# A convolution-attention block and a group-normed attention on one core: rows for the second attention's residual taken by transposing x1, GpSimd's sums dropped, and the third image's z_hat placed earlier

## The chip, the cores and the metric

One NeuronCore of a Trainium2 chip runs the whole kernel in one launch. The metric is the device time in microseconds (us), the median over the runs shown. The engines are named as in the profile: PE (TensorE, matrix products and transposes), PEld (its weight loads), DVE (VectorE), ACT (ScalarE), POOL (GpSimd), SP (SyncE, which issues the DMA transfers). Each engine works through its own list of instructions in order; semaphores make one engine wait for another.

## What is computed

The input x has 4 images of 16 x 16 pixels with 128 channels, all in float32. Two layers follow each other. The second half of the first layer and the second layer are what matters here:

```
# layer 0, after its deformable attention has given att
z    = att @ mo_w + mo_b + x
z_ln = layernorm(z, ln_g, ln_b)                    # per pixel, over 128 channels
x1   = gelu(z_ln @ mlp_w + mlp_b) + z
# layer 1
xg   = groupnorm(x1, 32 groups of 4 channels, per image) * gn_gamma + gn_beta
q, k, v = xg @ wq + bq, xg @ wk + bk, xg @ wv + bv
attn = softmax(q @ k.T / sqrt(128))                # 256 x 256 per image
out  = (attn @ v) @ wo + bo + x1
```

## The kernel before

All is written by hand, engine by engine, so the order of the text is the order of execution on each engine, and semaphores tie the engines together. An image is 256 pixels, that is two tiles of 128 pixels (rows on the partitions); there are 8 such tiles. The first attention runs tile by tile in a pipeline that takes until about 50 us of the span. What follows goes image by image, b = 0 to 3.

For each image: `z_tile` (L631) adds the projected attention and the input on DVE, with pixels on the partitions. `z_stats`, `z_aggr` and `z_var` (L636 to L646) take mean and variance over the channels, `z_scale` (L314) raises the variance to the power -1/2 on POOL, and `zhat_image` (L648) normalises two tiles on DVE. `z_transpose` (L1002) on PE transposes both z (columns 256 to 511 of a PSUM bank) and z_hat (columns 0 to 255) so that channels lie on the partitions; `zt_image` (L440) copies z_hat's transpose to SBUF on ACT, `mlp_image` (L1020) multiplies it by the MLP's weights, `gelu_image` (L444) applies gelu on ACT and gives gel_t, and `x1_image` (L653) on DVE adds the transposed z to it: x1_t, channels on the partitions.

Two users take x1. The group norm needs x1_t: `gn_stats`, `gn_aggr` on DVE, then on PE `gn_mean` (L1071), on DVE `gn_square` (L700), on PE `gn_spread` (L1083), on DVE `gn_var` (L706), on POOL `gn_pow` (L326), and on DVE `norm_image` (L712), which writes x_gn. This chain runs twice, for images 0 and 1 together (n = 0) and for images 2 and 3 (n = 1). From x_gn, `project_qk` (L1092) on PE and `project_out` (L719) on DVE make q and k.

The residual of the last line needs x1 with pixels on the partitions. Before, `gelu_transpose` (L1065) transposes gel_t back on PE, `residual` (L319) adds z and the output bias on POOL (z_res), and `x1_residual` (L658) on DVE adds the two: x1_res. It also frees the PSUM bank for q and k, so `project_qk(0)` and `(1)` wait for it, and `score_image(0)` and `(1)` (L1115) wait for x1_residual(2) and (3).

`keep_warm(2, 6)` (L812) issues two matmuls on a constant tile whose result nobody reads. The lists of calls that set the order stand at the end of each engine's block: L746 to L805 for DVE, L1150 on for PE, L332 to L345 for POOL. The bias sits in out_bias, written by ACT at L461.

Of the kernel before, what the change touches and what calls it, by code (L numbers as in the profile page):

```python
# [11 lines left out]
P = 128  # L12
B, H, W, C = 4, 16, 16, 128
HW = H * W
S = HW // P
T = B * S
# [52 lines left out]
def build(nc, x, early, fold, mid, late, rows, ln_rows, out):  # L69
    ctx = ExitStack()  # L70
    with ctx:
        def sb(name, shape, dt=F32):
            return ctx.enter_context(nc.sbuf_tensor(name, shape, dt))
# [25 lines left out]
        def r(name):  # L99
# [23 lines left out]
        out_bias = sb("out_bias", [P, C])  # L123
# [24 lines left out]
        z = sb("z", [P, T, C])  # L148
# [5 lines left out]
        z_t = sb("z_t", [P, T, P])  # L154
        gel_t = sb("gel_t", [P, B, HW])
        x1_t = sb("x1_t", [P, B, HW])
        z_res = sb("z_res", [P, T, C])
        x1_res = sb("x1_res", [P, T, C])
        gst = sb("gst", [P, B, 6])
        gmv = sb("gmv", [P, B, 2])  # L160
# [23 lines left out]
            "sampling": "coord_mm tanh_ok dx_ok dy_ok fx_ok ay_ok hx_ok hy_ok bilin_ok interp_mm sampled_ok",  # L184
            "queries, keys, values": "qh_mm qh_ok k_mm k_ok kblk_ok kblk_p v_mm v_even v_odd",
            "attention": """s_mm smax_ok ssub_ok pt_mm exp_ok av_mm recip_ok att_ok attt_mm attt_ok msa_mm xres_ok z_ok""",
            "norm of z and MLP": "zst_ok zmv_ok zve_ok zrs_ok zhat_ok zt_mm zt_ok mlp_mm gel_ok zres_ok x1t_ok gelt_mm x1res_ok",
            "group norm": "gst_ok gmv_ok dev_mm dev2_ok gvar_mm gve_ok gmean_ok grs_ok xgn_ok",
            "second attention": """qk_mm q1_ok k1_ok v1_mm v1_ok s1_mm nmax1_ok p1_ok p1t0_mm p1t1_mm p1t0_ok p1t1_ok
                av1_mm rec1_ok y_ok y_out""",  # L190
# [76 lines left out]
        @block.gpsimd  # L267
        def _(pool):
            pool.memset(warm[:, :], 0.0).then_inc(s["warm_set"], 1)  # L269
            pool.memset(ones_row[:, :], 1.0)  # L270
            pool.memset(ones_col[:, :], 1.0).then_inc(s["ones_set"], 1)
            pool.memset(eps[:, :], LN_EPS)
            pool.memset(neg_half[:, :], -0.5).then_inc(s["consts"], 1)
            pool.memset(v1[:, :, :, C:C + 1], 1.0).then_inc(s["v1ones_set"], 1)
            pool.memset(v_blk[:, :, :, 0:2 * HD], 0.0)
            pool.wait_ge(s["early_in"], 16)
            pool.wait_ge(s["hat_ok"], 4)
            for n in range(0, len(SHIFTS), WD_CHUNK):
                taps = w("dw_q")[:, n * PHASES:(n + WD_CHUNK) * PHASES]
                pool.tensor_tensor(wd[:, n:n + WD_CHUNK].rearrange("p n k j -> p (n k) j"),  # L280
                                   w("ident32").unsqueeze(1).to_broadcast([P, WD_CHUNK * PHASES, BLK]),
                                   taps.unsqueeze(2).to_broadcast([P, WD_CHUNK * PHASES, BLK]), ALU.mult).then_inc(s["wd_ok"], 1)

            def norm_affine(h):

                t = halves(h)

                pool.wait_ge(s["hat_a" if h else "hat_ok"], 4)
                pool.wait_ge(s["lnrow_in"], 16)
                pool.tensor_tensor(x_g[:, t], x_hat[:, t], gb[:, 0:C].unsqueeze(1).to_broadcast([P, 4, C]), ALU.mult).then_inc(s["xg_ok"], 1)  # L290
                pool.wait_ge(s["xg_ok"], h + 1)
                pool.tensor_tensor(x_ln[:, t], x_g[:, t], gb[:, C:2 * C].unsqueeze(1).to_broadcast([P, 4, C]), ALU.add).then_inc(s["xln_ok"], 1)

            norm_affine(0)
            pool.wait_ge(s["mid_in"], 16)
            pool.tensor_copy(v_blk[:, :, :, 2 * HD:VW],
                             w("ones_mask").unsqueeze(1).unsqueeze(1).to_broadcast([P, B, PAIRS, 2])).then_inc(s["vones_set"], 1)
            norm_affine(1)

            pool.wait_ge(s["bilin_ok"], G)  # L300
            pool.wait_ge(s["msabias_ok"], 1)
            pool.wait_ge(s["xst_in"], 16)
            pool.tensor_tensor(x_res[:, :, :], x_st[:, :, :].rearrange("p b (s c) -> p (b s) c", s=S),  # L303
                               msa_bias[:, :].unsqueeze(1).to_broadcast([P, T, C]), ALU.add).then_inc(s["xres_ok"], 1)

            for b in range(G, B):
                pool.wait_ge(s["k_ok"], 1)
                pool.tensor_tensor(k_blk[:, b], k_t[:, b].unsqueeze(1).to_broadcast([P, NH, PIX]),
                                   w("head_of").unsqueeze(2).to_broadcast([P, NH, PIX]), ALU.mult).then_inc(s["kblk_p"], 1)

            pool.wait_ge(s["late_in"], 16)
            pool.tensor_scalar(mlp_wg[:, :], w("mlp_w"), w("ln_g"), None, ALU.mult).then_inc(s["mlpw_ok"], 1)

            def z_scale(b):  # L314

                pool.wait_ge(s["zve_ok"], b + 1)
                pool.tensor_tensor(zrs[:, 2 * b:2 * b + 2], zve[:, 2 * b:2 * b + 2], neg_half[:, 0:2], ALU.pow).then_inc(s["zrs_ok"], 1)  # L317

            def residual(b):  # L319

                pool.wait_ge(s["z_ok"], 2 * b + 2)
                pool.wait_ge(s["outbias_ok"], 1)
                pool.tensor_tensor(z_res[:, 2 * b:2 * b + 2, :], z[:, 2 * b:2 * b + 2, :],
                                   out_bias[:, :].unsqueeze(1).to_broadcast([P, S, C]), ALU.add).then_inc(s["zres_ok"], 1)

            def gn_pow(n):  # L326

                i = slice(GN_SETS[n].start, GN_SETS[n].stop)
                pool.wait_ge(s["gve_ok"], n + 1)
                pool.tensor_tensor(grs[:, i], gve[:, i], neg_half[:, i], ALU.pow).then_inc(s["grs_ok"], 1)  # L330

            z_scale(0)  # L332
            pool.tensor_scalar(wq1g[:, :], w("wq1"), w("gn_gamma"), None, ALU.mult)
            pool.tensor_scalar(wk1g[:, :], w("wk1"), w("gn_gamma"), None, ALU.mult)
            pool.wait_ge(s["w_vo_ok"], 1)
            pool.tensor_scalar(w_vog[:, :], w_vo[:, :], w("gn_gamma"), None, ALU.mult).then_inc(s["gamma_ok"], 1)
            z_scale(1)
            residual(0)
            residual(1)
            z_scale(2)  # L340
            z_scale(3)
            gn_pow(0)
            residual(2)
            residual(3)
            gn_pow(1)  # L345

        @block.scalar
# [162 lines left out]
        def _(dve):  # L510
# [137 lines left out]
            def zhat_image(b):  # L648
                dve.wait_ge(s["zrs_ok"], b + 1)
                for i in (2 * b, 2 * b + 1):  # L650
                    dve.tensor_scalar(z_hat[:, i], z[:, i], zmv[:, i, 0:1], zrs[:, i:i + 1], ALU.subtract, ALU.mult).then_inc(s["zhat_ok"], 1)

            def x1_image(b):  # L653

                dve.wait_ge(s["gel_ok"], b + 1)
                dve.tensor_tensor(x1_t[:, b], gel_t[:, b], zt_bank(b)[:, HW:2 * HW], ALU.add).then_inc(s["x1t_ok"], 1)  # L656

            def x1_residual(b):  # L658
                dve.wait_ge(s["gelt_mm"], b + 1)
                dve.wait_ge(s["zres_ok"], b + 1)  # L660
                dve.tensor_tensor(x1_res[:, 2 * b:2 * b + 2], bank[3 + b][:, HW:2 * HW].rearrange("p (s c) -> p s c", s=S),
                                  z_res[:, 2 * b:2 * b + 2], ALU.add).then_inc(s["x1res_ok"], 1)

            max_tile(0)
            shift_tile(0)
# [26 lines left out]
            def gn_stats(b):  # L692
                dve.wait_ge(s["x1t_ok"], b + 1)
                dve.bn_stats(gst[:, b], x1_t[:, b]).then_inc(s["gst_ok"], 1)  # L694
# [62 lines left out]
            x1_image(0)  # L757
            z_tile(T - 2)
            x1_image(1)
            gn_stats(0)  # L760
            gn_stats(1)
            z_tile(T - 1)
# [5 lines left out]
            z_aggr(T - 1)  # L768
            z_var(3)
            gn_square(0)  # L770
            zhat_image(2)
            x1_residual(0)
            gn_var(0)
            zhat_image(3)

            norm_image(0)
            norm_image(1)
            x1_residual(1)
            x1_image(2)
            gn_stats(2)  # L780
            project_out(0)
            x1_residual(2)
            x1_image(3)
            gn_stats(3)
            gn_aggr(2)
            gn_aggr(3)
            x1_residual(3)
            gn_square(1)
            project_out(1)
            gn_var(1)  # L790
            max_image(0)
            norm_image(2)
# [15 lines left out]
        def _(pe):  # L808
# [253 lines left out]
                if i == 2:  # L1062
                    fold_second()

            def gelu_transpose(b):  # L1065
                pe.wait_ge(s["gel_ok"], b + 1)
                for t in range(S):
                    m = pe.transpose(bank[3 + b][:, HW + t * P:HW + (t + 1) * P], gel_t[:, b, t * P:(t + 1) * P], w("ident"))
                m.then_inc(s["gelt_mm"], 1)

            def gn_mean(n):  # L1071

# [116 lines left out]
            att_transpose(T - 1)  # L1189
            keep_warm(2, 6)  # L1190
            out_project(T - 1)
            gelu_transpose(0)
            gelu_transpose(1)
            keep_warm(2, 6)
            gn_mean(0)
            keep_warm(2, 6)
            gn_spread(0)
            z_transpose(2)
            z_transpose(3)
            mlp_image(2)  # L1200

            project_qk(0)
            mlp_image(3)
            gelu_transpose(2)
            project_v(0)
            gelu_transpose(3)
            project_qk(1)
            gn_mean(1)
            score_image(0)
            gn_spread(1)  # L1210
            project_v(1)
# [81 lines left out]
```

## Time and profile before

| | before |
|---|---|
| median of 3 runs | 79.3 us (78.77, 79.3, 79.84) |
| the profiled execution, its own time | 79.27 us |
| its span, first to last instruction | 77.4 us |
| PE busy | 70.6 us (91%) |
| DVE busy | 51.7 us (67%) |
| ACT busy | 33.9 us (44%) |
| POOL busy | 24.3 us (31%) |
| granted PE clock | 1.000 over the span |

The span is the time from the first to the last instruction in the trace; the execution's own time is 1.87 us more than that. A busy PE is not a PE at its peak: its matmuls are pipelined and overlap, so successive ones of 128 columns in float32 start 0.11 us apart though each lasts 0.27 us. A DVE instruction likewise starts a little before the record of the one ahead ends. In rows of a timeline several like instructions are merged ("x2"), and the time is from the first's start to the last's end. The name x_t in the trace is the tile x1_t, x_res stands for x_res and x1_res, q and k for q1 and k1, dev for dev2, and so on, since numbers are left out.

### The profile page before, as it was taken

The numbers are of one execution on the slowest core, as the hardware profiler recorded it, in microseconds if no ns is written. First come the engines' busy times: TensorE is split into PE (matmuls) and PEld (weight loads), VectorE is DVE, ScalarE is ACT, GpSimd is POOL, SyncE is SP. The second block draws the span as 40 slices with busy tenths as digits, with TensorE's granted clock in tenths as the row PEclk, the third lists the DMA queues.
The fourth block names the chain that finished last, engine by engine and source line by source line (L and its number), as shares of the span: only waits on it lengthen the run. The fifth ranks groups of instructions, "written<-read, shape, count | busy, mean of one in ns | idle before, by whom it ended". The sixth has DMA issues, their size and how long they took to land.

```text
span 77.4 us, 1968 instructions
## 1 busy us (share of the span) xinstructions
PE 70.6 (91%) x732; PEld 53.6 (69%) x732; DVE 51.7 (67%) x172; ACT 33.9 (44%) x84; POOL 24.3 (31%) x37
## 2 busy tenths in 40 slices
PE   4999699998999999999999999998897999998950
PEld 2345599783786647879777989845485869996830
DVE  0478742116366959477789968599799786868480
ACT  6112397068139563524424419820248048263600
POOL 5008999900000038390019137123820030000000
PEclk9999999999999999999999999999999999999999
DMA  0789870000000000000000000000000000010112
GB/s 9 226 270 150 305 289 12 0 8 0 0 8 0 0 0 4 0 0 8 0 0 0 4 0 0 8 0 0 0 0 0 0 0 4 0 68 9 59 55 89
DMA packets 3051, 3.07 MB, mean 40 GB/s; under 512 B 225, under 2 KB 2657, under 8 KB 3042
## 3 DMA queue, kind: packets, MB, share of 16 engines
q1 hardware_dynamic: 3042, 2.95, 12.8%
q8 instruction: 6, 0.10, 0.5%
q14 instruction: 3, 0.02, 0.1%
HBM read 2.42 MB, written 0.52 MB: 38 GB/s over the span
## 4 chain that ended last, share of the span: by engine, by line
PE 63%; DVE 17%; issue 5%; DMA 5%; ACT 3%; SPq 2%; POOL 2%; DVEq 0%; POOLq 0%; ACTq 0%
PE bank L810 53%; DMA x_hw<-x 5%; PE bank L971 5%; PE bank L1140 2%; DVE smax L604 2%; DVE x_t L656 1%; DVE gst L694 1%; SPq L247 1%; DVE st L528 1%; DVE bilin L578 1%; DVE x_gn L716 1%; DVE dist_y L562 1%; PE bank L989 1%; DVE q_conv L517 1%; POOL grs L330 1%
## 5 line engine op out<-in xcount | busy, mean ns | idle before, releaser
L810 PE MATMUL bank<-k_blk,qh 128*128 128x512 f32 x16 | 8.4, 605 | 0.0
L810 PE MATMUL bank<-v_blk,p_t 128*128 128x34 f32 x64 | 7.8, 267 | 0.0
L810 PEld LDWEIGHTS bank<-v_blk,p_t 128*128 128x128 f32 x64 | 7.8, 192 | 0.0
L810 PE MATMUL bank<-warm 128*128 128x512 bf16 x18 | 6.3, 471 | 1.0 <-POOL warm L269 1.0
L604 DVE TENSOR_REDUCE smax<-bank 128x8 f32<-128x512 f32 x8 | 5.5, 685 | 2.4 <-PE bank L810 2.4
L317 POOL TENSOR_TENSOR zrs<-zve,neg_half 128x2 f32<-128x2 f32 x4 | 2.9, 714 | 12.7 <-DVE zve L646 12.7
L810 PE MATMUL bank<-q_ph,wd 128*32 128x112 f32 (+5 forms) x256 | 6.8, 249 | 0.0
L303 POOL TENSOR_TENSOR x_res<-x_st,msa_bias 128x1024 f32<-128x1024 f32 x1 | 2.4, 2358 | 12.8 <-DVE bilin L578 12.8
L431 ACT ACTIVATE p_t<-bank 128x512 f32<-128x512 f32 x8 | 4.8, 597 | 3.4 <-PE bank L971 3.4
L810 PEld LDWEIGHTS bank<-q_ph,wd 128*32 128x32 f32 x256 | 5.6, 109 | 0.7 <-issue 0.3
L611 DVE TENSOR_TENSOR s_sub<-bank,smax 128x512 f32<-128x512 f32 x8 | 5.5, 682 | 0.1
L280 POOL TENSOR_TENSOR wd<-pack_early 128x512 f32<-128x512 f32 x4 | 4.1, 1046 | 4.4 <-DVE x_hat L540 4.4
L810 PE MATMUL bank<-v,p_t 128*128 128x129 f32 x32 | 4.8, 284 | 0.6 <-ACT p_t L233 0.4
L810 PEld LDWEIGHTS bank<-v,p_t 128*128 128x128 f32 x32 | 4.2, 190 | 1.2 <-issue 1.0
L971 PE MATMUL bank<-pack_early,s_sub 128*128 128x128 f32 x32 | 5.0, 279 | 0.0
L488 ACT ACTIVATE p<-bank,nmax 128x256 f32<-128x256 f32 x8 | 3.4, 476 | 3.0 <-DVE nmax L728 2.8
L438 ACT COPY att_t<-bank 128x128 f32<-128x128 f32 x8 | 2.1, 263 | 5.4 <-PE bank L989 5.3
L971 PEld LDWEIGHTS bank<-pack_early,s_sub 128*128 128x128 f32 x32 | 3.7, 144 | 0.8 <-issue 0.5
L810 PE MATMUL bank<-k,q 128*128 128x256 f32 x16 | 4.2, 385 | 0.0
L528 DVE BATCH_NORM_STATS2 st<-x_hw 128x6 f32<-128x128 f32 x8 | 1.8, 283 | 3.2 <-DMA x_hw<-x 3.2
L810 PEld LDWEIGHTS bank<-warm 128*128 128x128 bf16 x18 | 2.0, 122 | 2.9 <-issue 1.9
L810 PE MATMUL bank<-pack_mid,att_t 128*128 128x128 f32 x16 | 3.7, 311 | 0.2 <-DVE z L634 0.2
(149 smaller groups left out, 161.2 us busy)
## 6 DMA issues: line engine op xcount, KB each, us to landing
x_st<-x SPq DMA_DIRECT2D x1, 512.0 KB, 6.7
pack_late<-late SPq DMA_DIRECT2D x1, 448.0 KB, 7.3
out<-y SPq DMA_DIRECT2D x3, 128.0 KB, 1.7
pack_fold<-fold SPq DMA_DIRECT2D x1, 320.0 KB, 4.1
pack_mid<-mid SPq DMA_DIRECT2D x1, 261.0 KB, 5.8
x_hw<-x SPq DMA_DIRECT2D x2, 128.0 KB, 2.2
x_hw<-x SPq DMA_DIRECT2D x1, 256.0 KB, 3.8
pack_early<-early SPq DMA_DIRECT2D x1, 184.0 KB, 2.5
```

Of the source, the lines that this page charges most:

```text
L280: pool.tensor_tensor(wd[:, n:n + WD_CHUNK].rearrange("p n k j -> p (n k) j"), w("ident32").unsqueeze(1).to_broadcast([P, WD_CHUNK * PHASES ...
L303: pool.tensor_tensor(x_res[:, :, :], x_st[:, :, :].rearrange("p b (s c) -> p (b s) c", s=S), msa_bias[:, :].unsqueeze(1).to_broadcast([P, ...
L317: pool.tensor_tensor(zrs[:, 2 * b:2 * b + 2], zve[:, 2 * b:2 * b + 2], neg_half[:, 0:2], ALU.pow).then_inc(s["zrs_ok"], 1)
L431: act.activation(p_t[:, i % 2].rearrange("p j q -> p (j q)"), bank[5 + i % 2][:, :], ACT.Exp).then_inc(s["exp_ok"], 1)
L438: act.copy(att_t[:, i % 2], bank[0][:, 0:P]).then_inc(s["attt_ok"], 1)
L488: act.activation(p1[:, b % 2, t], bank[5 + b % 2][:, t * HW:(t + 1) * HW], ACT.Exp, bias=nmax1[:, 2 * b + t:2 * b + t + 1]).then_inc(s["p1 ...
L528: dve.bn_stats(st[:, i], x_hw[:, i]).then_inc(s["stats"], 1)
L604: dve.tensor_reduce(smax[:, i % 2], scores(i), AX.X, ALU.max).then_inc(s["smax_ok"], 1)
L611: dve.tensor_tensor(s_sub[:, i % 2], scores(i), smax[:, i % 2].unsqueeze(2).to_broadcast([P, NH, PIX]), ALU.subtract).then_inc(s["ssub_ok" ...
L810: return pe.matmul(o, l, r_, start=start, stop=stop, **k)
L971: m = pe.transpose(bank[5 + i % 2][:, j * P:(j + 1) * P], s_sub[:, i % 2, 2 * j:2 * j + 2].rearrange("p h q -> p (h q)"), w("ident"))
L1140: m = pe.transpose(bank[(2, 0)[t]][:, j * P:(j + 1) * P], p1[:, b % 2, t, j * P:(j + 1) * P], w("ident"))
```

## The change

Three things are changed; no other line moves.

- `residual` is gone from POOL, and z_res with it. `gelu_transpose` becomes `x1_transpose`: PE transposes x1_t, not gel_t, and so has to wait for x1_image on DVE, not for gelu on ACT. `x1_residual` adds out_bias, broadcast over the two tiles.
- On DVE `zhat_image(2)` moves from behind `gn_square(0)` to ahead of `gn_stats(0)`; `x1_image(2)` moves from behind `x1_residual(1)` to ahead of `norm_image(0)`; `x1_residual(2)` and `x1_residual(3)` move behind `gn_aggr(3)` and `project_out(1)`.
- On PE `z_transpose(2)` goes ahead of `gn_mean(0)`, `mlp_image(2)` ahead of `gn_spread(0)`, in the place of one `keep_warm(2, 6)`; `mlp_image(3)` goes ahead of `project_qk(0)`; the transposes of images 2 and 3 for the residual go behind `project_v(0)` and `gn_mean(1)`.

```
-            def residual(b):
-                pool.wait_ge(s["z_ok"], 2 * b + 2)
-                pool.wait_ge(s["outbias_ok"], 1)
-                pool.tensor_tensor(z_res[:, 2 * b:2 * b + 2, :], z[:, 2 * b:2 * b + 2, :],
-                                   out_bias[:, :].unsqueeze(1).to_broadcast([P, S, C]), ALU.add).then_inc(s["zres_ok"], 1)
             z_scale(1)
-            residual(0)
-            residual(1)
             z_scale(2)
             z_scale(3)
             gn_pow(0)
-            residual(2)
-            residual(3)
             gn_pow(1)
...
             def x1_residual(b):
-                dve.wait_ge(s["gelt_mm"], b + 1)
-                dve.wait_ge(s["zres_ok"], b + 1)
+                dve.wait_ge(s["x1rows_mm"], b + 1)
+                dve.wait_ge(s["outbias_ok"], 1)
                 dve.tensor_tensor(x1_res[:, 2 * b:2 * b + 2], bank[3 + b][:, HW:2 * HW].rearrange("p (s c) -> p s c", s=S),
-                                  z_res[:, 2 * b:2 * b + 2], ALU.add).then_inc(s["x1res_ok"], 1)
+                                  out_bias[:, :].unsqueeze(1).to_broadcast([P, S, C]), ALU.add).then_inc(s["x1res_ok"], 1)
...
-            def gelu_transpose(b):
-                pe.wait_ge(s["gel_ok"], b + 1)
+            def x1_transpose(b):
+                pe.wait_ge(s["x1t_ok"], b + 1)
                 for t in range(S):
-                    m = pe.transpose(bank[3 + b][:, HW + t * P:HW + (t + 1) * P], gel_t[:, b, t * P:(t + 1) * P], w("ident"))
-                m.then_inc(s["gelt_mm"], 1)
+                    m = pe.transpose(bank[3 + b][:, HW + t * P:HW + (t + 1) * P], x1_t[:, b, t * P:(t + 1) * P], w("ident"))
+                m.then_inc(s["x1rows_mm"], 1)
...
             x1_image(1)
+            zhat_image(2)
             gn_stats(0)
```

Three places in the order of instructions. First PE between the transposes for the residual of images 0 and 1 and the fourth image's z_hat. Before:

```order
L1068 MATMUL bank<-pack_early,gel_t 128x128 x4
L810 MATMUL bank<-warm 128x512 x2
L810 MATMUL bank<-gmv,pack_late 128x2
L810 MATMUL bank<-warm 128x512 x2
L810 MATMUL bank<-gmv,pack_late 128x2
L810 MATMUL bank<-dev,pack_late 128x2
L810 MATMUL bank<-gmv,pack_late 128x2
L1014 MATMUL bank<-pack_early,z 128x128 x2
L1017 MATMUL bank<-pack_early,z_hat 128x128 x2
```

The same place of the change:

```order
L1055 MATMUL bank<-pack_early,x_t 128x128 x4
L797 MATMUL bank<-warm 128x512 x2
L1001 MATMUL bank<-pack_early,z 128x128 x2
L1004 MATMUL bank<-pack_early,z_hat 128x128 x2
L797 MATMUL bank<-gmv,pack_late 128x2
L797 MATMUL bank<-z_t,mlp_wg 128x256
L797 MATMUL bank<-gmv,pack_late 128x2
L797 MATMUL bank<-dev,pack_late 128x2
L797 MATMUL bank<-gmv,pack_late 128x2
L1001 MATMUL bank<-pack_early,z 128x128 x2
L1004 MATMUL bank<-pack_early,z_hat 128x128 x2
L797 MATMUL bank<-z_t,mlp_wg 128x256
```

The third image's transposes and MLP now stand on both sides of the first group norm matmul (gmv), and the second pair of warm matmuls is gone.

Second, PE around the first projection to q and k (x_gn with wq1g and wk1g) up to the first scores (k,q). Before:

```order
L810 MATMUL bank<-x_gn,wq1g 128x256
L810 MATMUL bank<-x_gn,wk1g 128x256
L810 MATMUL bank<-z_t,mlp_wg 128x256
L1068 MATMUL bank<-pack_early,gel_t 128x128 x2
L810 MATMUL bank<-w_vog,x_gn 128x128 x2
L1068 MATMUL bank<-pack_early,gel_t 128x128 x2
L810 MATMUL bank<-x_gn,wq1g 128x256
L810 MATMUL bank<-x_gn,wk1g 128x256
L810 MATMUL bank<-gmv,pack_late 128x2
L810 MATMUL bank<-k,q 128x256 x2
```

The same place of the change, from the fourth image's MLP on:

```order
L797 MATMUL bank<-z_t,mlp_wg 128x256
L797 MATMUL bank<-x_gn,wq1g 128x256
L797 MATMUL bank<-x_gn,wk1g 128x256
L797 MATMUL bank<-w_vog,x_gn 128x128 x2
L1055 MATMUL bank<-pack_early,x_t 128x128 x2
L797 MATMUL bank<-x_gn,wq1g 128x256
L797 MATMUL bank<-x_gn,wk1g 128x256
L797 MATMUL bank<-gmv,pack_late 128x2
L1055 MATMUL bank<-pack_early,x_t 128x128 x2
L797 MATMUL bank<-k,q 128x256 x2
```

The fourth image's MLP moved ahead of x_gn's first product, and the last transpose moved behind the second group norm matmul, directly ahead of the scores.

Third, DVE from the variance of the last two z tiles (zve) to the first q. Before:

```order
L646 TENSOR_SCALAR zve<-zmv 128x2
L704 TENSOR_SCALAR dev<-bank 128x1 x2
L651 TENSOR_SCALAR z_hat<-z,zmv,zrs 128x128 x2
L661 TENSOR_TENSOR x_res<-bank,z_res 128x256
L709 TENSOR_SCALAR gve<-bank 128x2
L710 COPY gmean<-bank 128x2
L651 TENSOR_SCALAR z_hat<-z,zmv,zrs 128x128 x2
L716 TENSOR_SCALAR x_gn<-x_t,gmean,grs 128x256 x2
L661 TENSOR_TENSOR x_res<-bank,z_res 128x256
L656 TENSOR_TENSOR x_t<-gel_t,bank 128x256
L694 BN_STATS gst<-x_t 128x6
L722 TENSOR_SCALAR q<-bank,cols 128x256
```

The same place of the change:

```order
L634 TENSOR_SCALAR zve<-zmv 128x2
L692 TENSOR_SCALAR dev<-bank 128x1 x2
L649 TENSOR_TENSOR x_res<-bank,out_bias 128x256
L697 TENSOR_SCALAR gve<-bank 128x2
L698 COPY gmean<-bank 128x2
L639 TENSOR_SCALAR z_hat<-z,zmv,zrs 128x128 x2
L644 TENSOR_TENSOR x_t<-gel_t,bank 128x256
L704 TENSOR_SCALAR x_gn<-x_t,gmean,grs 128x256 x2
L649 TENSOR_TENSOR x_res<-bank,out_bias 128x256
L682 BN_STATS gst<-x_t 128x6
L710 TENSOR_SCALAR q<-bank,cols 128x256
```

The first z_hat pair of this list left for a place seven rows further up, and the third image's x_t came ahead of x_gn.

## Rows read from the trace of the kernel before

**Rows 1.** The page: PE's busy time, and its granted clock in 40 slices.
```profile
PE 70.6 (91%) x732; PEld 53.6 (69%) x732; DVE 51.7 (67%) x172; ACT 33.9 (44%) x84; POOL 24.3 (31%) x37
PEclk9999999999999999999999999999999999999999
```

**Rows 2.** The chain that ended last, in order: start us, us, what.
```profile
54.47 0.80 POOL grs L330
...
56.02 0.81 DVE x_gn L716
...
57.87 0.47 DVE q L722
...
60.12 3.33 PE bank L810 x20
...
63.46 0.80 PE bank L1140 x4
...
72.39 0.22 PE bank L1140 x2
```

**Rows 3.** Timeline, z_hat, z_res and x_gn: start us, us, engine, line, op [idle before].
```profile
46.09 1.12 DVE L651 TENSOR_SCALAR z_hat<-z,zmv,zrs 128x128 f32<-128x128 f32 x2 [0.64 <-POOL zrs L317]
...
46.40 1.41 POOL L323 TENSOR_TENSOR z_res<-z,out_bias 128x256 f32<-128x256 f32 x2 [0.34 <-ACT out_bias L461]
...
47.93 0.38 PE L1017 MATMUL bank<-pack_early,z_hat 128*128 128x128 f32 x2
...
55.22 1.45 POOL L323 TENSOR_TENSOR z_res<-z,out_bias 128x256 f32<-128x256 f32 x2
...
55.36 1.46 DVE L716 TENSOR_SCALAR x_gn<-x_t,gmean,grs 128x256 f32<-128x256 f32 x2 [0.40 <-POOL grs L330]
...
63.12 0.73 DVE L716 TENSOR_SCALAR x_gn<-x_t,gmean,grs 128x256 f32<-128x256 f32 x2 [0.22 <-POOL grs L330]
```

**Rows 4.** DVE's groups, first x_gn of each pair: xcount | busy us, mean ns | idle.
```profile
L716 DVE TENSOR_SCALAR x_gn<-x_t,gmean,grs 128x256 f32<-128x256 f32 x1 | 0.7, 731 | 0.4 <-POOL grs L330 0.4
...
L716 DVE TENSOR_SCALAR x_gn<-x_t,gmean,grs 128x256 f32<-128x256 f32 x1 | 0.4, 412 | 0.2 <-POOL grs L330 0.2
```

**Rows 5.** Timeline of the first group norm, 50 to 54.4 us.
```profile
50.06 0.70 POOL L317 TENSOR_TENSOR zrs<-zve,neg_half 128x2 f32<-128x2 f32 x1 [2.26 <-DVE zve L646]
...
50.84 0.41 DVE L656 TENSOR_TENSOR x_t<-gel_t,bank 128x256 f32<-128x256 f32 x1
...
52.02 0.24 DVE L698 BATCH_NORM_AGGREGATE gmv<-gst 128x2 f32<-128x6 f32 x2
...
52.96 0.34 DVE L704 TENSOR_SCALAR dev<-bank 128x1 f32<-128x1 f32 x2
...
53.23 0.59 DVE L651 TENSOR_SCALAR z_hat<-z,zmv,zrs 128x128 f32<-128x128 f32 x2
...
54.23 0.16 DVE L709 TENSOR_SCALAR gve<-bank 128x2 f32<-128x2 f32 x1
```

**Rows 6.** Timeline from the fourth image's z_hat to the first scores.
```profile
54.37 0.59 DVE L651 TENSOR_SCALAR z_hat<-z,zmv,zrs 128x128 f32<-128x128 f32 x2
...
55.02 0.44 PE L1017 MATMUL bank<-pack_early,z_hat 128*128 128x128 f32 x2
...
56.15 0.70 PE L810 MATMUL bank<-x_gn,wq1g 128*128 128x256 f32 x2 [0.26 <-DVE x_gn L716]
...
56.30 0.36 ACT L442 COPY z_t<-bank 128x256 f32<-128x256 f32 x1
...
56.68 0.59 PE L810 MATMUL bank<-x_gn,wk1g 128*128 128x256 f32 x2
...
57.08 0.40 DVE L656 TENSOR_TENSOR x_t<-gel_t,bank 128x256 f32<-128x256 f32 x1
57.12 0.59 PE L810 MATMUL bank<-z_t,mlp_wg 128*128 128x256 f32 x2
...
58.64 0.41 DVE L661 TENSOR_TENSOR x_res<-bank,z_res 128x256 f32<-128x256 f32 x1
```

More of the change, by code:

```diff
@@ L156, in build @@
         x1_t = sb("x1_t", [P, B, HW])
-        z_res = sb("z_res", [P, T, C])
         x1_res = sb("x1_res", [P, T, C])
@@ L186, in build @@
             "attention": """s_mm smax_ok ssub_ok pt_mm exp_ok av_mm recip_ok att_ok attt_mm attt_ok msa_mm xres_ok z_ok""",
-            "norm of z and MLP": "zst_ok zmv_ok zve_ok zrs_ok zhat_ok zt_mm zt_ok mlp_mm gel_ok zres_ok x1t_ok gelt_mm x1res_ok",
+            "norm of z and MLP": "zst_ok zmv_ok zve_ok zrs_ok zhat_ok zt_mm zt_ok mlp_mm gel_ok x1t_ok x1rows_mm x1res_ok",
             "group norm": "gst_ok gmv_ok dev_mm dev2_ok gvar_mm gve_ok gmean_ok grs_ok xgn_ok",
@@ L770, in _ @@
             gn_square(0)
-            zhat_image(2)
             x1_residual(0)
@@ L774, in _ @@
             zhat_image(3)
+            x1_image(2)
             norm_image(0)
@@ L778, in _ @@
             x1_residual(1)
-            x1_image(2)
             gn_stats(2)
             project_out(0)
-            x1_residual(2)
             x1_image(3)
@@ L786, in _ @@
             gn_aggr(3)
-            x1_residual(3)
+            x1_residual(2)
             gn_square(1)
             project_out(1)
+            x1_residual(3)
             gn_var(1)
@@ L1191, in _ @@
             out_project(T - 1)
-            gelu_transpose(0)
-            gelu_transpose(1)
+            x1_transpose(0)
+            x1_transpose(1)
             keep_warm(2, 6)
+            z_transpose(2)
             gn_mean(0)
-            keep_warm(2, 6)
+            mlp_image(2)
             gn_spread(0)
-            z_transpose(2)
             z_transpose(3)
-            mlp_image(2)
+            mlp_image(3)
             project_qk(0)
-            mlp_image(3)
-            gelu_transpose(2)
             project_v(0)
-            gelu_transpose(3)
+            x1_transpose(2)
             project_qk(1)
             gn_mean(1)
+            x1_transpose(3)
             score_image(0)
```

## The prediction

> **What bounds the kernel now.** I read the page's parts first: PE is busy for 91% of the span at full granted clock [rows 1]. A busy PE says little here, so the chain that ended last comes next. The reader is to see where it changes engine. Up to about 50 us it is PE, from 60.12 us on PE again, in pieces of 3.33 and 0.80 us with nothing between them [rows 2]. Between the two it runs over DVE and POOL: grs, x_gn, q, then PE's 60.12. The change works in these ten microseconds, and behind 60.12 us it alters nothing but one transpose pair. So I ask when the matmul that starts at 60.12 us (gn_mean(1), the first of the 20) starts after the change, and what stands between it and the first scores. The timeline gives the times.
>
> **POOL's sums.** The four z_res of `residual` go. POOL itself waits most of the time, so their time on POOL is worth nothing. What they do to DVE is: the z_hat pair that runs beside z_res takes 1.12 us, a pair without it 0.59 [rows 3, 5]; the x_gn pair beside z_res takes 1.46 us, the later pair 0.73 [rows 3], the first of each pair 731 and 412 ns [rows 4]. The Trainium skill, page "SBUF — State Buffer", tells that VectorE and GpSimd share one pair of ports, which an instruction of the tensor_scalar kind in its two-port form takes for its whole length, so that the other blocks; by that rule the slowing ends with the sums, and the trace agrees (1.46 against 0.73 us).
>
> Where is it on the path? The z_hat pair at 46.09 us ends at 47.21, and PE takes it only at 47.93 [rows 3]: 0.72 us of slack, worth nothing. The x_gn pair lies on the chain: 0.73 us less for the pair, 0.32 for its first (0.731 − 0.412).
>
> **z_hat(2) moves ahead of the group norm.** It needs zrs, ready at 50.76 (50.06 + 0.70), and it stands behind x1_image(1), which ends at 51.25 [rows 5]: no new wait. Two z_hat take 0.59 us less an overlap of 0.09, so 0.50 us. Behind it are queued gn_stats, gn_aggr (gmv), z_stats, z_var and gn_square (dev), with PE waiting for gmv and dev. DVE has no gap there, so all of it comes 0.50 us later: gmv at 52.76, dev over at 53.80 instead of 53.30. On PE, z_transpose(2) (four products 0.11 apart, 0.44 us) starts behind the warm matmuls at about 52.1 and is over by 52.8, when gmv arrives: free. mlp_image(2) needs two products of 0.22 us and an ACT copy (0.36) between 52.8 and 53.8: it fits ahead of gn_spread(0), which waits for dev. So gve starts at 54.73 instead of 54.23, and grs (0.80 us long) is ready at 55.76 instead of 55.26 [rows 2, 5].
>
> **What DVE does beside grs.** DVE was idle for 0.40 us ahead of x_gn [rows 3]. Now z_hat(3) (54.87 to 55.46) and x1_image(2) (0.33 of its own, to 55.79) fill the wait for grs. x_gn(0) runs from 55.86, with 0.10 for the semaphore as now, to 56.27, x_gn(1) to 56.60. Before, the two ended at 56.09 (55.36 + 0.731) and 56.83 (56.02 + 0.81) [rows 2 to 4]. The first is 0.18 later, the second 0.23 earlier.
>
> **The fourth image on PE.** mlp_image(3) now stands ahead of project_qk(0) in PE's queue. Its inputs: z_hat(3) is over at 55.46 instead of 54.96; PE's transposes run from 55.52 to 55.96 (before 55.02, 0.44 long); the ACT copy takes 0.36 behind that, to 56.37; mlp starts at 56.43 and takes 0.44 of PE, the distance from 56.68 to 57.12 [rows 6]. So project_qk(0) does not start at 56.32, when x_gn(0) would let it, but at 56.87, against 56.15 now. Its two products took from 56.15 to 57.27 (56.68 + 0.59); packed, 0.44 + 0.59, they end at 57.90 [rows 6]. Behind this wait stand project_v(0), the transposes for image 2, project_qk(1) and gn_mean(1) on PE, and project_out(0) on DVE.
>
> **DVE up to the second group norm.** x1_residual(1) and gn_stats(2) are over by 57.25, since x1_image(2) is already done. project_out(0) then waits for PE and starts at about 57.95 instead of 57.87: DVE, which was the bound, now idles 0.7 us, and here most of what x_gn gave back is lost. From there to gmv nothing differs but x1_residual(2), moved behind gn_aggr(3): 0.33 us less (58.64 to 58.97, where x1_image(3) began) [rows 6]. gn_mean(1) comes at 60.12 + 0.08 − 0.33 = 59.87.
>
> **Behind gn_mean(1).** The transpose pair of x1_t for image 3 now lies directly ahead of score_image(0). It costs 0.22 us, like any pair of transposes [rows 2]. Before, the pair stood where PE waited for DVE anyway, so nothing is given back for it. score_image(0) also waits for x1_residual(2), over at 60.14, which this covers. Net: −0.25 + 0.22 = −0.03 us. x1_residual(3), moved behind project_out(1), is over at about 61.8, and score_image(1), which waits for it, starts after 62.3. The rest repeats what it was.
>
> **Edits at nothing.** x1_residual adds out_bias instead of z_res: again one PSUM and one SBUF operand of the same size, 0.41 us [rows 6]. Bounds: 0 and, if the broadcast cost as much as the 0.32 us that the sharing cost, +0.3 for each of two that PE waits for. I take 0, by the nearest row. x1_transpose(0) and (1) wait for x1_image, over at 50.72 and 51.25; PE reaches them at 51.3 and 51.5 behind out_project(7): covered by 0.2 us. The two warm matmuls that go filled a wait: worth nothing while the clock stays.
>
> **Sum.** −0.03 us; against the profiled execution's own 79.27 us that is 79.24, 0.06 below the median of the runs shown (79.3). I say 79.2.
>
> **Rivals.**
>
> *More is kept (faster).* If z_hat(3), its copy and mlp_image(3) ran 0.4 us earlier, project_qk(0) would start at 56.32 and project_out(0) at 57.49 (56.32 + 0.53 + 0.59 + 0.05), 0.46 us sooner, and all behind it follows: 79.24 − 0.46 = 78.8. For it: ACT is idle there and copies take 0.36 at once. Against: z_hat(3) stands behind gn_var(0), which is 0.50 late. The ceiling, if all slowing of DVE by POOL lay on the path, is 0.53 + 0.73 = 1.26 us, so 78.0; that is still less than 2%.
>
> *The queues lose more (slower).* z_hat(2)'s 0.50 us runs through to gn_mean(1), and the transpose pair's 0.22 comes on top. The place is project_qk(0) behind mlp_image(3): beyond 56.87 us each later start reaches project_out(0) one for one, since DVE is then idle. It decides from 0.03 us of further delay on. An ACT copy or PE's transposes late by 0.3 to 0.5 us give 79.5 to 79.8. For it: three hand-overs (DVE to PE, PE to ACT, ACT to PE) now lie in a row ahead of project_qk(0), where none did. Against: each has its price in the rows, and I counted them.
>
> *The clock falls (slower).* Two of the warm matmuls go, and PE now waits at 55.0 to 55.5, 55.96 to 56.43 and about 59.1 to 59.8. The granted clock is full in all slices [rows 1], also through the waits from 53.2 to 56.2 and at 59.6 to 60.1. If it fell to the lower level through one stretch such as the 3.33 us piece [rows 2], this piece would take twice as long: 79.24 + 3.3 = 82.5. The Trainium skill, page "TensorE: Matmul & The Clock Gate", Part 4, states that transposes do not keep the clock up as matmuls do, which speaks against putting transposes where warm matmuls were. By that rule this rival would come true; the trace does not test it, since no stretch at the low level is in it.
>
> **Numbers.** Forecast (79.0 to 79.5) 0.55; more is kept (78.4 to 79.0) 0.20; the queues lose more (79.5 to 80.1) 0.20; the clock 0.04; an unnamed gain beyond 78 0.01. The range leaves out the ends: 78.5 to 80.0; the likeliest case's own is 79.0 to 79.5. It takes in the bound of x1_residual (+0.6 at most, 79.8). Two per cent, about what a measurement of this kernel tells from no change, is 1.6 us, that is 77.7 and 80.9. Only the unnamed gain passes the one, only the clock and a rest of the queues the other: faster 0.02, same 0.93, slower 0.05.
>
> **What the profile of the change would show.** x_gn's pair about 0.73 us long both times; z_hat(2) right behind x1_image(1), and gmv near 52.8; grs ending near 55.8 without an idle DVE ahead of x_gn; PE's mlp(3) directly ahead of wq1g at 56.4 and 56.9; DVE idle for about 0.7 us ahead of the first q; gn_mean(1) near 59.9, and the scores near 60.3. Wrong would be: x_gn still at 0.7 or 0.8 us each (the sharing was not the cause), a clock below 1.000, or the first q before 57.6 or after 58.2.

## The result and the profile after the change

| | before | after |
|---|---|---|
| median | 79.34 us (4 runs, 78.77 to 79.84) | 80.62 us (4 runs, 80.14 to 81.83) |
| ratio after / before | | 1.014, 95% interval 1.009 to 1.019 |
| profiled execution: span, granted PE clock | 77.4 us, 1.000 | 80.0 us, 0.956 |

The change made the kernel 1.4% slower. The forecast was 79.2 us with a range of 78.5 to 80.0, so the time lies outside. Ratios here and below leave out executions more than 1.5% above the fastest of their kernel, here the one of 81.83 us. The profiled execution of the change is the slowest of its four (81.83 us), so a second trace, of an execution of 80.7 us, is read beside it (e9_change_again, below). The other three of the four had a granted clock of 0.974, 0.974 and 0.978 over their spans.

The page of the changed kernel, busy time and granted clock in 40 slices of 2 us:

```profile
PE 73.0 (91%) x730; PEld 55.7 (70%) x730; DVE 50.5 (63%) x172; ACT 33.9 (42%) x84; POOL 21.4 (27%) x33
...
PEclk9999999999999999999999999999555899999999
```

The row of fives is what the kernel before does not have [rows 1]: from 55.9 to 62.7 us (read in stretches of 0.2 us) TensorE ran at the lower of its two levels, 1.2 GHz instead of 2.4. The chain that ended last (start us, us, what) shows what this did:

```profile
55.06 0.16 DVE gve L697
...
55.28 0.52 DVE z_hat L639 x2
...
55.85 0.70 PE bank L1004 x2
...
56.58 0.38 ACT z_t L430
...
57.00 3.78 PE bank L797 x10
60.78 0.43 PE bank L1055 x2
61.21 1.78 PE bank L797 x6
62.99 0.27 PE bank L1055 x2
63.27 2.85 PE bank L797 x18
66.11 0.01 issue
66.12 0.80 PE bank L1127 x4
```

Before, the ten microseconds up to 60.12 lay on DVE and POOL [rows 2]. Now ten matmul instructions from 57.00 on (five float32 products, each recorded as two) take 3.78 us and stand on the chain themselves. The timeline of the same kernel gives single instructions (start us, us, engine, line, op, shapes, idle before):

```profile
56.19 0.73 DVE L704 TENSOR_SCALAR x_gn<-x_t,gmean,grs 128x256 f32<-128x256 f32 x2
...
57.00 1.22 PE L797 MATMUL bank<-z_t,mlp_wg 128*128 128x256 f32 x2 [0.46 <-ACT z_t L430]
...
58.02 1.06 PE L797 MATMUL bank<-x_gn,wq1g 128*128 128x256 f32 x2
...
58.87 1.06 PE L797 MATMUL bank<-x_gn,wk1g 128*128 128x256 f32 x2
...
59.97 0.48 DVE L710 TENSOR_SCALAR q<-bank,cols 128x256 f32<-128x256 f32 x1 [2.37 <-PE bank L797]
...
62.71 0.28 PE L797 MATMUL bank<-gmv,pack_late 128*128 128x2 f32 x2
```

The x_gn pair takes 0.73 us, as forecast, where it took 1.46 [rows 3]. But the first product to q and the one to k now start 0.85 us apart (58.02 and 58.87), where they had started 0.53 us apart (56.15 and 56.68 [rows 6]; 0.43 us in e1_fill below, at full clock). DVE idles 2.37 us ahead of the first q, and gn_mean(1) comes at 62.71 us, not at 59.87 as forecast.

For comparisons between kernels I take as zero the start of the add for the last z tile but one. DVE makes it at 50.64 us before and at 50.96 here. Of what the change touches only the first two sums on GpSimd lie ahead of it, and they leave no mark on it: in the three traces with the sums it stands at 50.64 to 51.35 us, in the ten without at 50.27 to 51.63. Times counted from it leave this spread out. The start of the first transposes of the softmax (L1140 before, 63.46 us [rows 2]) is then at 12.82 us before and at 15.16 after.

### The profile page after: what moved, and what is told of

It reads as the page before. It is cut to its first block, busy times and chain, and to the rows that moved or that the text cites. A ratio compares the mean times of both kernels' runs of the same rounds, so it can differ in the third digit from the quotient of the medians.

```text
span 80.0 us, 1956 instructions
## 1 busy us (share of the span) xinstructions
PE 73.0 (91%) x730; PEld 55.7 (70%) x730; DVE 50.5 (63%) x172; ACT 33.9 (42%) x84; POOL 21.4 (27%) x33
## 4 chain that ended last, share of the span: by engine, by line
PE 75%; DVE 10%; ACT 4%; DMA 4%; issue 3%; SPq 1%; DVEq 0%; ACTq 0%
PE bank L797 63%; PE bank L958 4%; DMA x_hw<-x 4%; PE bank L1127 2%; PE bank L1004 2%; DVE smax L592 2%; PE bank L1055 1%; DVE q_conv L505 1%; DVE bilin L566 1%; DVE dist_y L550 1%; PE bank L976 1%; ACT z_t L430 1%; DVE s_sub L599 1%; PE bank L1001 1%; DVE z_hat L639 1%
## 5 line engine op out<-in xcount | busy, mean ns | idle before, releaser
L797 PE MATMUL bank<-q_ph,wd 128*32 128x84 f32 (+5 forms) x256 | 6.4, 249 | 0.0
L710 DVE TENSOR_SCALAR q<-bank,cols 128x256 f32<-128x256 f32 x4 | 1.9, 482 | 3.7 <-PE bank L797 3.7
L322 POOL TENSOR_TENSOR grs<-gve,neg_half 128x2 f32<-128x2 f32 x2 | 1.5, 740 | 9.5 <-DVE gve L697 9.5
```

The lines of the kernel that those rows point to most:

```text
L710: dve.tensor_scalar(q1[:, b], bank[3 + b % 2][:, 0:HW], cols1[:, 0:1], C ** -0.5, ALU.add, ALU.mult).then_inc(s["q1_ok"], 1)
L797: return pe.matmul(o, l, r_, start=start, stop=stop, **k)
```

## The experiments

Eleven kernels were run in three jobs, each beside the kernel before on the same chip; one job ran on chip 7, the other two on chip 12. The chip of the first four executions of the change, those of the result, is not on record. "Fallen" are executions whose granted clock over the span is 0.978 or lower (all others have 0.993 or more); "zero to transposes" is the stretch just defined, in the profiled execution.

| kernel | chip | median us | ratio to before, 95% | fallen | zero to transposes |
|---|---|---|---|---|---|
| before | 7 and 12 | 79.41 to 79.43 | | 0 of 31 and 0 of 60 | 12.82 |
| e1_fill | 7 | 79.59 | 1.001 (0.997 to 1.004) | 0 of 10 | 12.84 |
| e2_pair_back | 7 | 79.31 | 0.999 (0.995 to 1.003) | 0 of 10 | 13.13 |
| e3_before_minus_pair | 7 | 79.61 | 1.002 (0.998 to 1.007) | 1 of 10 | 12.83 |
| e4_no_sums | 7 | 78.64 | 0.990 (0.986 to 0.994) | 0 of 10 | 12.18 |
| e5_transposes | 12 | 80.58 | 1.004 (0.998 to 1.010) | 4 of 10 | 13.14 (at full clock) |
| e6_rows_old_order | 12 | 79.15 | 0.995 (0.991 to 0.999) | 0 of 12 | 12.19 |
| e7_fill_transpose_early | 12 | 79.48 | 1.000 (0.996 to 1.004) | 0 of 12 | 12.84 |
| e8_mlp_back | 12 | 80.20 | 0.998 (0.991 to 1.005) | 8 of 10 | 13.71 (fallen) |
| e9_change_again | 12 | 80.64 | 1.000 (0.994 to 1.006) | 7 of 10 | 14.21 (fallen) |
| e10_before_minus_both | 12 | 79.98 | 1.004 (1.000 to 1.009) | 7 of 10 | 14.45 (fallen) |
| e11_rows_residual_late | 12 | 78.74 | 0.992 (0.988 to 0.996) | 0 of 9 | 12.02 |

The ratios of e5, e8 and e9 leave out all or nearly all of their fallen executions, that of e10 two of seven, so for these four the median and the count of the fallen say more. The time of an execution alone does not tell whether the clock fell in it: one of e2 took 80.64 us and two of e5 took 80.49 and 80.72 with the clock held.

**Is it the clock, or the queue?** Two theories were open: A, the whole loss is the clock; B, the fourth image's MLP ahead of project_qk(0) costs by itself.

```
                     pe.transpose(zt_bank(b)[:, HW + t * P:HW + (t + 1) * P], z[:, 2 * b + t], w("ident"))
+                if b == 3:
+                    keep_warm(3, 6)
                 pe.wait_ge(s["zhat_ok"], 2 * b + 2)
...
             z_transpose(3)
+            keep_warm(2, 6)
             mlp_image(3)
```

> The changed kernel with five warm matmuls more on PE: three between the z and the z_hat transposes of the fourth image (where PE waited 0.55 to 0.8 us for z_hat), two ahead of mlp_image(3) (where it waited 0.46 us for the ACT copy). They fill waits only. Theory A (the clock fell because PE had too little to do from 52.7 to 57.0 us, and that is the whole loss): granted clock 1.00, no stretch at the low level, gn_mean(1) near 60.0 us, time as the kernel before within 0.3 us (79.1 to 79.6). Theory B (the fourth image's MLP ahead of project_qk(0) is what costs, the clock comes on top): clock 1.00, but DVE still idles over 1.2 us ahead of the first q and the time stays at 80 us or more.

The granted clock on the page of e1_fill:

```profile
PEclk9999999999999999999999999999999999999999
```

The first q in its timeline:

```profile
58.44 0.48 DVE L710 TENSOR_SCALAR q<-bank,cols 128x256 f32<-128x256 f32 x1 [0.76 <-PE bank L797]
```

Theory A holds. With PE's two waits filled, the clock stays up in all ten executions, DVE idles 0.76 us (forecast: 0.7) instead of 2.37, and the time is that of the kernel before. Theory B wanted 80 us. This settles the loss against the kernel before; it does not say that the new place of the MLP is free, since the dropped sums gain at the same time (e4, e6 and e8 below). These ten ran on chip 7; e7 below has the same filling on chip 12, where the unfilled change falls in most executions (next), and none of its 12 fell.

**The unaltered change once more.** No edit.

> The changed kernel, unaltered, on the same chip as the two below, to count how often the clock falls and to have a trace of a typical execution. If the fall is a matter of chance with a rate near one: 9 or 10 of 10 executions at 0.970 to 0.980 and about 80.6 us; if its rate is that of e8_mlp_back (8 of 10), some at 1.00 and those near 79.2 us.

Seven of ten fell, at 80.47 to 81.11 us; the three that did not took 79.05, 79.64 and 79.64. So the same program has two times, with medians of 80.7 and 79.6 us: 1.1 us apart by the clock, though the second rests on three executions. With the first four executions 11 of 14 have fallen. Stretches of 2 us in the trace of e9 (bounds, length, busy time of PE, PEld, DVE, ACT, POOL, then the granted clock):

```profile
54.00:56.00 2.00, 1.45 (x11) 1.01 (x10) 1.34 (x7) 0.48 (x1) 1.20 (x2) 1.00 0.00 0
56.00:58.00 2.00, 1.54 (x5) 1.22 (x5) 1.36 (x4) 0.61 (x2) 0.00 (x0) 0.59 0.00 0
58.00:60.00 2.00, 2.00 (x9) 1.72 (x8) 0.53 (x2) 0.24 (x1) 0.00 (x0) 0.55 0.00 0
60.00:62.00 2.00, 1.78 (x12) 1.33 (x11) 1.81 (x8) 1.66 (x2) 0.00 (x0) 1.00 0.00 0
```

The same stretches of the kernel before:

```profile
54.00:56.00 2.00, 1.78 (x12) 1.14 (x11) 1.52 (x6) 0.44 (x2) 1.53 (x3) 1.00 0.00 0
56.00:58.00 2.00, 1.85 (x11) 1.65 (x12) 1.97 (x6) 0.92 (x3) 0.68 (x1) 1.00 0.00 0
```

PE was busy for 1.45 us of 54 to 56 where it had been busy for 1.78, and no warm matmuls came after 52.5 us; then the clock fell, at 56.4 us, and came back at 59.8 us, after 3.4 us. In the slower execution shown above it stayed low for 6.8 us, from 55.9 to 62.7. The fall in e9 costs 14.21 − 12.84 = 1.37 us against e1_fill, in which the clock held. In 3.4 us at half speed PE does what takes 1.7 us at full speed, so it loses 1.7 us; the 0.3 us that don't reach the path go mostly into its waits, such as the one for gmv ahead of gn_mean(1), which is 0.45 us in e1_fill and 0.22 in e9. In the slower execution 15.16 − 12.84 = 2.32 us of 3.4 lost reach the path.

**Which part of the change lets it fall?** The dropped pair was put back where it had stood, and, the other way round, dropped from the kernel before.

```
             mlp_image(2)
+            keep_warm(2, 6)
             gn_spread(0)
```

> The changed kernel with the dropped pair of warm matmuls put back, between mlp_image(2) and gn_spread(0), where PE waits 0.28 us for dev. The pair takes 0.43 us, so gn_spread(0) comes at most 0.15 us later. If the missing pair alone let the clock fall: clock 1.00, 79.3 to 79.7. If the waits behind it do (0.79 and 0.86 us of idle weight loads ahead of z_hat and of mlp_image(3)): the clock still falls, 80.3 to 80.9.

```
             gn_mean(0)
-            keep_warm(2, 6)
             gn_spread(0)
```

> The kernel before without the pair of warm matmuls between gn_mean(0) and gn_spread(0); nothing else. If the pair's absence alone lets the clock fall, the clock is below 1.00 here too and the time 80.3 to 81.8. If it takes the longer waits of the changed order, clock 1.00 and 79.3 within 0.2 us.

With the pair put back the clock held (0 of 10 fallen), although both waits behind it stay (0.56 and 0.46 us). It costs more than I expected: gve comes 0.28 us later than in e1_fill counted from zero (4.38 against 4.10), not 0.15. With the pair dropped from the kernel before, one of ten executions fell. Read with e9, this says that neither the missing pair nor the waits alone take the clock, and that both together do in most executions. But e2 and e3 ran on chip 7 and e9 on chip 12, and no execution of the change is known to have run on chip 7; that it is the pair, and not the chip, which makes 0 and 1 of ten out of seven is likely and not shown.

PE's busy time alone does not tell the cases apart either. In the trace of e2, whose clock held:

```profile
54.00:56.00 2.00, 1.33 (x11) 0.85 (x9) 1.28 (x6) 0.21 (x2) 0.79 (x1) 1.00 0.00 0
```

Zero lies 0.44 us earlier in e2 than in e9. Counted from it, PE is busy for 1.62 us from 3 to 5 us in e2 and for 1.45 in e9, and from 4 to 6 us for 1.06 and 0.98. How little is too little, no run here measures.

```
             z_transpose(3)
-            mlp_image(3)
             project_qk(0)
+            mlp_image(3)
             project_v(0)
```

> The changed kernel with mlp_image(3) behind project_qk(0) again; no warm matmuls added. If the wait for the copy ahead of mlp_image(3) is what lets the clock fall: clock 1.00 and, with project_out(0) 0.4 us earlier, 78.9 to 79.2. If PE's thin work before it is enough: the clock falls still and the time stays at 80 us or more.

Eight of ten fell; the two that did not took 78.67 and 79.20 us. The place of the fourth image's MLP is not the cause of the fall, then: with it back, PE waits for x_gn instead of the copy, and the stretch ahead is as thin (1.39 us of 54 to 56). It does cost time of its own: project_qk(0) starts 5.70 us after zero in e8, ahead of the fall, and 6.33 us after zero in e1_fill.

```
             gelu_transpose(1)
-            keep_warm(2, 6)
             gn_mean(0)
-            keep_warm(2, 6)
             gn_spread(0)
```

> The kernel before without both last pairs of warm matmuls (the one behind the transposes of images 0 and 1, and the one between gn_mean(0) and gn_spread(0)). Its order and its sums on GpSimd are untouched, so only PE's work in 51.8 to 53.4 us is thinner. If the clock goes by how much matmul work stands in this stretch, whatever the order: it falls in most executions and the time is 80.3 us or more in them. If the changed order of the queues is needed for the fall: 1 of 10 at most, 79.4 us.

Seven of ten fell, at 79.76 to 81.17 us, the others took 79.21 to 79.61; of the kernel before, none of 25 in the same job on the same chip fell. The order of the rest and the GpSimd sums were those of before. The trace of a fallen execution:

```profile
52.00:54.00 2.00, 0.99 (x7) 0.84 (x6) 1.97 (x14) 0.00 (x0) 0.73 (x1) 0.94 0.00 0
54.00:56.00 2.00, 2.00 (x11) 2.00 (x11) 1.14 (x6) 0.33 (x1) 1.04 (x2) 0.50 0.00 0
```

PE busy for 0.99 of 2 us, and the clock at the lower level directly behind. No reordering is needed for the fall; taking PE's warm matmuls out of this stretch is enough.

**Do transposes hold the clock as warm matmuls do?** The pair of e2 as four transposes of the same 0.44 us:

```
             mlp_image(2)
+            for j in range(4):
+                pe.transpose(bank[6][:, j * P:(j + 1) * P], z[:, j], w("ident"))
             gn_spread(0)
```

> The pair put back as before e2_pair_back, but as four float32 transposes of z into the same bank (4 x 0.11 = 0.44 us, the length of the pair of warm matmuls) instead of two warm matmuls. If any work of PE at this place holds the clock: clock 1.00 and 79.3 to 79.7, as with the warm pair. If transposes do not count for the clock (Part 4 of the Trainium skill's page TensorE: Matmul & The Clock Gate): the clock falls as in the changed kernel, 0.96 to 0.98 over the span, 80.3 to 81.5.

Inconclusive. Four of ten fell with the transposes, none of ten with warm matmuls in their place (on the other chip), 7 of 10 with neither. Four against none leans towards the rule of the Trainium skill (page "TensorE: Matmul & The Clock Gate", Part 4: PE-mode transpose) that transposes do not keep the clock up as matmuls do; four against seven leans the other way. Both can be chance, and the first can be the chip. The median, 80.58 us, rests in part on the two executions of 80.49 and 80.72 us whose clock held; the profiled one, of 80.49 us, is late by its zero (51.63 us) already.

**What the sums on GpSimd cost.** The kernel before without the sums; the output bias is left out of its result.

```
-            residual(0)
-            residual(1)
...
-            residual(2)
-            residual(3)
...
-                dve.wait_ge(s["zres_ok"], b + 1)
+                dve.wait_ge(s["z_ok"], 2 * b + 2)
...
-                                  z_res[:, 2 * b:2 * b + 2], ALU.add)
+                                  z[:, 2 * b:2 * b + 2], ALU.add)
```

> The kernel before without the four sums on GpSimd: x1_residual adds z itself (the output bias is left out of the result), order and everything else as before. Isolates what the sums cost DVE. Sharing theory: x_gn pair 0.73 us instead of 1.46, z_hat pair at 46 us 0.59 instead of 1.12; x_gn(0) lets PE start project_qk(0) 0.32 us earlier, x_gn(1) ends 0.73 us earlier and with it the DVE chain to gmv: project_out(0) bound by PE from 56.95 on instead of DVE, so gn_mean(1) 0.5 to 0.7 us earlier and 78.6 to 78.8 us. If the sums do not matter: x_gn pair still 1.46, 79.3.

The timeline of e4_no_sums:

```profile
55.77 0.74 DVE L712 TENSOR_SCALAR x_gn<-x_t,gmean,grs 128x256 f32<-128x256 f32 x2 [0.40 <-POOL grs L330]
```

Same place, same idle time ahead of it, 0.74 us instead of 1.46 [rows 3]. gn_mean(1) comes 8.84 us after zero instead of 9.48, and the transposes 0.64 us earlier; 78.64 us, 1.0% faster. The sums on GpSimd did slow DVE, and 0.64 of these 0.73 us lay on the path.

**The rows from x1 without the new order.** e6 is the first part of the change with full output, with both warm pairs and in the order of before but for one pair of transposes:

```
-            gelu_transpose(3)
             project_qk(1)
+            gelu_transpose(3)
             gn_mean(1)
```

> The first part of the change alone: the four sums on GpSimd go, the rows come from transposing x1, out_bias is added on DVE; all queues in the order of before with both warm pairs, but the transpose for image 3 stands behind project_qk(1), ahead of gn_mean(1), where PE waits 0.6 us for gmv. Full result. Sharing theory: as e4_no_sums, x_gn pair 0.73 us, gn_mean(1) 0.6 us earlier against the start of z's add, clock 1.00, 78.5 to 78.9. If waiting for x1_image instead of gelu costs PE something: 79.0 to 79.4.

Zero to transposes is 12.19 us, as without the sums (12.18): transposing x1_t instead of gel_t costs nothing. The ratio is 0.995 (0.991 to 0.999); the median, 79.15 us, is above the 78.9 that I had allowed.

Beside e1_fill this shows what the new order of the queues costs while the clock holds: 12.84 − 12.19 = 0.65 us, which is all that the dropped sums give. It can be followed at the start of project_qk(0), counted from zero: 5.19 us in e6, 5.70 in e8, where z_hat(2) has moved ahead (0.51 us later), and 6.33 in e1_fill, where mlp_image(3) has moved ahead too (0.63 us more).

The last kernel, e11, is e6 with two of DVE's additions placed as in the change:

```
             project_out(0)
-            x1_residual(2)
             x1_image(3)
             gn_stats(3)
             gn_aggr(2)
             gn_aggr(3)
-            x1_residual(3)
+            x1_residual(2)
             gn_square(1)
             project_out(1)
+            x1_residual(3)
```

> e6_rows_old_order with x1_residual(2) behind gn_aggr(3) and x1_residual(3) behind project_out(1), as in the change. gn_mean(1) comes 0.33 us earlier against the start of z's last add but one; the scores, which wait for x1_residual(2), only 0.1 to 0.2 us earlier. Time 0.1 to 0.2 us under e6's, 78.9 to 79.0. If the scores' wait takes it all: the same as e6.

As expected: counted from zero, gn_mean(1) comes at 8.52 instead of 8.85 us, the scores at 8.93 instead of 9.10, the transposes at 12.02 instead of 12.19. At 78.74 us, ratio 0.992 (0.988 to 0.996), this version is faster than both kernels of the case, by 0.8% against the kernel before. Whether it is faster than e6 the times don't tell, since their intervals overlap; by one trace of each it is 0.17 us.

**The last transpose.** e1_fill with x1_transpose(3) moved ahead of gn_mean(1):

```
             project_qk(1)
+            x1_transpose(3)
             gn_mean(1)
-            x1_transpose(3)
             score_image(0)
```

> e1_fill with the last transpose pair (x1_transpose(3)) ahead of gn_mean(1) instead of behind it. My term says the place behind costs 0.22 us on the path and the place ahead costs nothing, since PE waits there for gmv: the scores of image 0 start 0.2 us earlier relative to gn_mean(1), 79.2 where e1_fill had 79.4 to 79.6. If the pair was hidden by the wait for x1_residual(2), nothing changes.

The rows of PE in e1_fill, then in e7:

```profile
60.38 0.38 PE L797 MATMUL bank<-gmv,pack_late 128*128 128x2 f32 x2 [0.45 <-DVE gmv L686]
60.62 0.42 PE L1057 MATMUL bank<-pack_early,x_t 128*128 128x128 f32 x2
60.88 1.03 PE L797 MATMUL bank<-k,q 128*128 128x256 f32 x4
61.74 0.28 PE L797 MATMUL bank<-gmv,pack_late 128*128 128x2 f32 x2
```

```profile
59.29 0.38 PE L1057 MATMUL bank<-pack_early,x_t 128*128 128x128 f32 x2
59.90 0.38 PE L797 MATMUL bank<-gmv,pack_late 128*128 128x2 f32 x2 [0.23 <-DVE gmv L686]
60.32 1.10 PE L797 MATMUL bank<-k,q 128*128 128x256 f32 x4
61.26 0.28 PE L797 MATMUL bank<-gmv,pack_late 128*128 128x2 f32 x2
```

From gn_mean(1) to the next gmv product it is 1.36 us in both, so the pair costs nothing there. Without it the scores start 0.42 us behind gn_mean(1), where they start 0.24 us behind it in the kernel before: they wait for x1_residual(2). e11 against e6 shows the same without the pair: x1_residual(2) moved behind gn_aggr(3) lengthens the way from gn_mean(1) to the next gmv product from 1.19 to 1.35 us.

## Why the prediction was wrong

- **The sharing of DVE with GpSimd: right.** x_gn 0.73 us for the pair, forecast 0.73, and shown to be the sums' doing by e4. The additions with out_bias, put at nothing, did cost nothing (0.41 us each).
- **z_hat(2) ahead of the group norm, 0.50 us later for all behind it: right.** gve starts 4.11 us after zero in e9 and 3.59 before: 0.52.
- **The wait for grs filled: right.** No idle time stands ahead of x_gn any more.
- **The fourth image on PE: right.** mlp_image(3) was to start 5.79 us after zero (56.43 − 50.64), and starts at 5.80 in e9.
- **The first q:** forecast 7.31 us after zero; at held clock 7.39 (e1). gn_mean(1): forecast 9.23, 9.33 in e1, 9.48 before. Both terms are 0.1 us short.
- **The transpose pair for 0.22 us behind gn_mean(1): wrong,** it costs nothing (e7). I had the wait for x1_residual(2) covered by the pair; it is the pair that is covered. The wait costs 0.17 us (1.36 against 1.19 us to the next gmv product), which takes up the 0.15 that gn_mean(1) gained: the size was nearly right, the reason was not.
- **The sum:** −0.03 us forecast, +0.02 us measured from zero to the transposes at held clock (12.84 in e1 against 12.82). The sum of the queues was forecast well, in part because two misses cancel: gn_mean(1) came 0.1 us late, and the way behind it cost 0.05 us less than forecast. The three executions of e9 that kept the clock lie inside the range.
- **The failed step: "worth nothing while the clock stays".** The two warm matmuls were costed at nothing, and the clock's fall was put in as a rival with a chance of 0.04. It happened in 11 of 14 executions. I argued from the full clock of the kernel before, through its waits; but these waits had the second warm pair among them. The change took that pair away and made the wait for z_hat longer, to 0.55 us of idle PE (the weight loads' wait grew from 0.35 to 0.79 us), in the very stretch behind it. The prediction had this wait and the one for the copy within 0.1 us (55.0 to 55.5 and 55.96 to 56.43); what it had wrong was that they are free. With them filled, 0 of 10 and 0 of 12 executions fell (e1, e7). e10 shows how near the edge the kernel before stands: without its two pairs, 7 of 10 executions fall.
- **The price of this rival: wrong too.** I had 3.3 us for one stretch, taking 3.33 us of PE's work at full speed for what the stretch holds, and all of it as on the path. The low stretch of e9 lasts 3.4 us as it runs, which is 1.7 us of such work, and 1.37 of it reach the path; in the times it is 1.1 us. Even the low stretch twice as long, in the first trace of the change, costs 2.32.

Of the other rivals, "more is kept" did not come about, and "the queues lose more" neither (e1: 12.84 against 12.82 before).

## What to carry to other kernels

Warm matmuls that fill a wait are not always free to take away: their price can be the clock of the stretch behind them, and an untroubled clock in the trace before says only that it holds with them. Whoever removes or reorders PE's work in a stretch in which PE waits for other engines should count what is left for PE there and give the fall of the clock a serious chance. Take the parts of such a change one by one: here dropping the sums on GpSimd alone was worth 0.64 us; the new order of the queues took 0.65 us back while the clock held, and with one pair of warm matmuls less it cost the clock in most executions.

## What the runs showed of the hardware

- The fall of the clock is a matter of chance from one execution to the next: the same program fell in 7 of 10 executions on one chip (e9), and the medians of its fallen and its other executions are 1.1 us apart. With few executions the median of a kernel can stand on either.
- It fell without any long wait of PE: in the two traces of the changed kernel the one wait over 0.2 us ahead of the fall, back to 44 us, is 0.55 us long (for z_hat), and in e9 the clock fell within the next, of 0.46 us (for the copy); in e10 the longest ahead of it is 0.66 us.
- Once it had fallen it stayed low for 3.4 us in the traces of e8 and e9 and for 6.8 us in those of e10 and of the change's first job; the latter with PE busy without a break from 57.00 to 62.7 us.
- A DVE pair of 0.73 us takes 1.46 us beside GpSimd sums in float32, though the two work on different tiles (x_gn before and in e4).
